# The residual of each FFN pair's first chunk turned by VectorE's 32x32 blocks and two transfers instead of by TensorE

## What is computed

```python
x = x + attn(layernorm(x) * ln_g + ln_b)     # q, k times a normalised sigmoid gate, relu()**2 + eps,
                                             # causal running sums k (x) v and k over the sequence
z = layernorm(x)                             # "z1" below; the part that the change is about
P = z @ U1                                   # 512 -> 128
H = gelu(P @ V1 + b1)                        # 128 -> 2048
x = x + (H @ U2) @ V2 + b2                   # 2048 -> 128 -> 512
```

## Time and profile before

| | us |
|---|---|
| median of 3 runs | 1702.19 (1701.56 to 1702.4) |
| the profiled execution | 1701.4 |
| its span, from the first to the last instruction | 1699.7 |
| PE busy | 1668.6 |
| DVE busy | 1437.1 |
| POOL busy | 880.5 |
| ACT busy | 629.6 |

### The profile page before, as it was taken

One profiled execution on the slowest core, in us unless ns is written; L12 is line 12 of the kernel. 1 busy time (PEld: TensorE's weight loads), 2 busy tenths in 40 slices (PEclk: granted clock), 3 DMA queues, 4 the chain that ended last, 5 costly groups with the idle time before them and its releaser, 6 DMA issues.

```text
span 1699.7 us, 39613 instructions
## 1 busy us (share of the span) xinstructions
PE 1668.6 (98%) x16221; PEld 1404.5 (83%) x16221; DVE 1437.1 (85%) x2223; ACT 629.6 (37%) x1178; POOL 880.5 (52%) x1026
## 2 busy tenths in 40 slices
PE   6899999999999999999999999999999999999997
PEld 4688888888888888888888888888888888888886
DVE  6888888888888888888888888888888888888885
ACT  4233334333433433433433333333333334334333
POOL 3355555555555555555555555555555555555540
PEclk9999999999999999999999999999999999999999
DMA  8323333333332233242243233333323333323310
GB/s 224 93 58 64 65 75 46 70 75 57 71 70 47 74 71 60 73 64 53 74 72 58 74 46 70 75 59 70 73 45 73 70 60 73 71 47 72 60 45 26
DMA packets 206324, 115.67 MB, mean 68 GB/s; under 512 B 151144, under 2 KB 161792, under 8 KB 206144
## 3 DMA queue, kind: packets, MB, share of 16 engines
q1 hardware_dynamic: 205280, 111.57, 31.6%
q10 hardware_dynamic: 864, 1.57, 0.4%
HBM read 79.38 MB, written 33.72 MB: 67 GB/s over the span
## 4 chain that ended last, share of the span: by engine, by line
PE 93%; DVE 3%; DMA 1%; issue 1%; SPq 1%; ACT 0%; POOL 0%; DVEq 0%; POOLq 0%
PE ps_a L849 11%; PE ps_a L850 10%; PE ps_a L851 10%; PE scores L849 8%; PE scores L851 8%; PE scores L850 8%; PE ps_h L849 4%; PE ps_h L850 4%; PE ps_h L851 4%; PE scores L980 4%; PE scores L1016 4%; PE ps_q L849 3%; PE ps_q L850 3%; PE ps_q L851 3%; PE scores L856 3%; PE scores L1010 2%
## 5 line engine op out<-in xcount | busy, mean ns | idle before, releaser
L447 POOL TENSOR_TENSOR h_lo<-h_full,h_hi 128x512 fp32r<-128x512 f32 x244 | 318.0, 1309 | 233.7 <-DVE h_hi L665 233.7
L849 PE MATMUL ps_a<-wx_hi,zt_hi 128*128 128x512 f32 x768 | 315.7, 411 | 6.6 <-DVE key_sums L787 4.2
L850 PE MATMUL ps_a<-wx_lo,zt_hi 128*128 128x512 f32 x768 | 305.1, 397 | 0.0
L851 PE MATMUL ps_a<-wx_hi,zt_lo 128*128 128x512 f32 x768 | 305.1, 397 | 0.0
L530 ACT ACTIVATE h_full<-ps_h,cols 128x256 f32<-128x256 f32 x512 | 204.0, 475 | 149.7 <-PE ps_h L851 149.6
L665 DVE CAST h_hi<-h_full 128x512 fp32r<-128x512 f32 x256 | 193.5, 766 | 22.9 <-ACT h_full L530 15.8
L849 PEld LDWEIGHTS ps_a<-wx_hi,zt_hi 128*128 128x128 f32 x768 | 145.3, 189 | 43.4 <-DVE zt_lo L620 7.4
L851 PEld LDWEIGHTS ps_a<-wx_hi,zt_lo 128*128 128x128 f32 x768 | 145.1, 189 | 35.6
L850 PEld LDWEIGHTS ps_a<-wx_lo,zt_hi 128*128 128x128 f32 x768 | 145.3, 189 | 28.7 <-issue 0.5
L541 ACT ACTIVATE query_t<-scores 128x512 f32<-128x512 f32 x64 | 38.3, 598 | 345.4 <-PE scores L856 345.4
L401 POOL TENSOR_TENSOR small<-moments,eps_col 128x1 f32<-128x1 f32 x64 | 12.2, 190 | 278.6 <-DVE moments L822 278.6
(11 more groups left out here) (156 smaller groups left out, 4133.2 us busy)
## 6 DMA issues: line engine op xcount, KB each, us to landing
xs<-L_attn_x SPq DMA_DIRECT2D x64, 256.0 KB, 4.1
key_blocks<-zs SPq DMA_DIRECT2D x64, 256.0 KB, 2.0
key_t<-key_blocks SPq DMA_DIRECT2D x256, 64.0 KB
out<-x1s SPq DMA_DIRECT2D x64, 256.0 KB, 2.1
xt<-x_turned SPq DMA_DIRECT2D x63, 256.0 KB, 4.2
key_sums<-carry_rows SPq DMA_DIRECT2D x60, 256.0 KB, 3.8
rows<-turned_rows SPq DMA_DIRECT2D x63, 64.0 KB, 4.5
x1s<-L_attn_W_gate SPq DMA_DIRECT2D x4, 256.0 KB, 4.1
```

The source lines that it names most:

```text
L447: E.tensor_tensor(h_lo[:, i % SLOTS, :], h_full[:, i % SLOTS, :], h_hi[:, i % SLOTS, :].bitcast(F32), ALU.subtract).then_inc(s["h_lo_ready ...
L849: E.matmul(ps, wh, mh, start=start and i == 0, stop=False)
L850: E.matmul(ps, wh, ml, start=False, stop=False)
L851: mm = E.matmul(ps, wl, mh, start=False, stop=stop and i == last)
```

## The change

In even steps, where d is the first chunk of a pair, TensorE no longer turns zs. VectorE turns zs by blocks of 32x32 into `queries`, which is free from the transposes of c until the query chain of n; SP stores that to a new buffer in memory (`res_dram`), waits, and gathers the blocks back into zs by four transfers of 128-byte pieces, so that the channels lie on the partitions. ScalarE makes x1t_hi from zs behind its gelus, and VectorE makes x1t_lo from zs behind the denominators and ahead of the first residual sum. New waits: VectorE's query chain waits for the store out of `queries`; SP waits for the block transposition and for its own store; ScalarE for the gathers. The key blocks go through `gate` instead of zs, and so the wait for their store moves from z1 (L830) to the denominators (L794). Odd steps keep the old way.

```diff
+    def pair(self, per=1):
+        return per * ((4 * self.p + self.off) // 2 + 1)
...
 # SP
             def step(p, b):
                 if isinstance(p, int) and 4 * p + b < 2:
                     load_tiles((range(FIRST + 6, FIRST + 9), range(FIRST + 9, len(tiles)))[b])
+                d = Chunk(p, b - 2)
+                if d.exists and d.half == 0:
+                    sp.wait_ge(s["res_ready"], d.pair())
+                    for j in range(HPG):
+                        wait(sp, res_in[j], d.pair(16) - 16)
+                    sp.dma_start(res_dram, queries[:, :]).then_inc(s["res_out"], 16)
+                    sp.wait_ge(s["res_out"], d.pair(16))
+                    for j in range(HPG):
+                        sp.dma_start(zs[j * HEAD:(j + 1) * HEAD, :].rearrange("d (f a t) -> d f a t", f=KT, t=HEAD),
+                                     res_dram.rearrange("(a d) (f j t) -> j d f a t", d=HEAD, f=KT, t=HEAD)[j])\
+                            .then_inc(res_in[j], 16)
...
-                    sp.dma_start(blocks_dram, zs[:, :]).then_inc(s["blocks_out"], 16)
+                    sp.dma_start(blocks_dram, gate[:, :]).then_inc(s["blocks_out"], 16)
 # ScalarE
-                if d.exists:
-                    act.wait_ge(s["tx_done"], d.done())
+                if d.exists and d.half:
+                    act.wait_ge(s["tx_done"], d.pair())
                     E.activation(x1t_hi[:, :, d.half * P:(d.half + 1) * P],
                                  ps_t[:, :].rearrange("p (k n) -> p k n", k=KT), ACT.Copy)\
                         .then_inc(s["x1t_hi_ready"], 1)
...
                     gelu(ffn, pairs[2])
                     gelu(ffn, pairs[3])
+                if d.exists and d.half == 0:
+                    for j in range(HPG):
+                        act.wait_ge(res_in[j], d.pair(16))
+                    E.activation(x1t_hi[:, :, 0:P], zs[:, :].rearrange("p (k n) -> p k n", k=KT), ACT.Copy)\
+                        .then_inc(s["x1t_hi_ready"], 1)
 # VectorE
+                def x1t_from_bank():
+                    if d.half:
+                        x1t_tail(ps_t)
+                def turn_residual():
+                    if d.exists and d.half == 0:
+                        dve.wait_ge(s["z1_ready"], d.done())
+                        if c.exists:
+                            dve.wait_ge(s["tq_done"], c.done())
+                        E.transpose(queries[:, :], zs[:, :]).then_inc(s["res_ready"], 1)
...
                         .then_inc(s["gate_evac"], 1)
+                    turn_residual()
...
                     squared_relu(n, s["key_done"], s["key_steps"], ps_b, KEY, keys[:, n.half, :],
-                                 x1t_tail)
+                                 x1t_from_bank)
...
+                    if d.exists and d.half == 0:
+                        dve.wait_ge(s["res_out"], d.pair(16))
                     squared_relu(n, s["query_done"], s["query_steps"], ps_a, QUERY, queries[:, :])
...
-                    if d.exists:
-                        dve.wait_ge(s["tx_done"], d.done())
-                    elif c.exists:
-                        dve.wait_ge(s["blocks_out"], c.done(16, 16))
-                    else:
-                        dve.wait_ge(s["tz_done"], 1)
-                    E.transpose(zs[:, :], keys[:, n.half, :]).then_inc(s["blocks_ready"], 1)
+                    E.transpose(gate[:, :], keys[:, n.half, :]).then_inc(s["blocks_ready"], 1)
...
                     dve.wait_ge(s["query_steps"], n.done(3, 3))
+                    dve.wait_ge(s["blocks_out"], n.done(16, 16))
                     E.scalar_tensor_tensor(out=gate[:, :], in0=queries[:, :], scalar=EPS, in1=key_sums[:, :],
...
+                if d.half == 0:
+                    x1t_tail(zs)
                 if c.exists:
                     dve.wait_ge(s["y_done"], c.done())
...
-                    if d.exists:
-                        dve.wait_ge(s["tx_done"], d.done())
+                    if d.exists and d.half:
+                        dve.wait_ge(s["tx_done"], d.pair())
...
-                    if n.exists:
-                        dve.wait_ge(s["blocks_out"], n.done(16, 16))
 # TensorE
-                if d.exists:
+                if d.exists and d.half:
                     pe.wait_ge(s["z1_ready"], d.done())
...
                     transpose4(zs, s["tx_done"])
...
-                    if d.exists:
+                    if d.exists and d.half:
                         pe.wait_ge(s["x1t_ready"], d.done())
```

More of the change, by code:

```diff
@@ L108, in block_kernel @@
 def block_kernel(nc, x, ln_g, ln_b, w_qkv, b_qkv, w_gate, b_gate, w_proj, b_proj,
-                 u1, v1, b1, u2, v2, b2, x_turned, out, carry_dram, rows_dram, blocks_dram):
+                 u1, v1, b1, u2, v2, b2, x_turned, out, carry_dram, rows_dram, blocks_dram, res_dram):
     ctx = ExitStack()
@@ L207, in block_kernel @@
             query_done query_steps value_done value_ready
-            sums_done den_steps blocks_ready blocks_out tq_done query_t_ready
+            sums_done den_steps blocks_ready blocks_out res_ready res_out tq_done query_t_ready
             scores_done probs_ready state_done state_ready ot_done ot_hi_ready ot_ready
@@ L215, in block_kernel @@
         xt_in = [sem(f"xt_in{i}") for i in range(4)]
+        res_in = [sem(f"res_in{j}") for j in range(HPG)]
         key_t_in = [sem(f"key_t_in{j}") for j in range(HPG)]
@@ L573, in step @@
                     gelu(ffn, pairs[3])
+                if d.exists and d.half == 0:
[3 more added lines that the diff above has]
+                        .then_inc(s["x1t_hi_ready"], 1)
+                if ffn.exists:
                     if b % 2 == 0:
@@ L677, in step, with x1t_tail @@
                 finishing = is_last(p)
-                def x1t_tail():
+                def x1t_tail(turned):
                     if d.exists:
@@ L682, in x1t_tail @@
                         part = slice(d.half * P, (d.half + 1) * P)
-                        E.tensor_tensor(x1t_lo[:, :, part], ps_t[:, :].rearrange("p (k n) -> p k n", k=KT),
+                        E.tensor_tensor(x1t_lo[:, :, part], turned[:, :].rearrange("p (k n) -> p k n", k=KT),
                                         x1t_hi[:, :, part].bitcast(F32), ALU.subtract).then_inc(s["x1t_ready"], 1)
+                def x1t_from_bank():
[7 more added lines that the diff above has]
+                        E.transpose(queries[:, :], zs[:, :]).then_inc(s["res_ready"], 1)
                 if n.exists:
@@ L704, in step @@
                     squared_relu(n, s["key_done"], s["key_steps"], ps_b, KEY, keys[:, n.half, :],
-                                 x1t_tail)
+                                 x1t_from_bank)
                 else:
-                    x1t_tail()
+                    turn_residual()
+                    x1t_from_bank()
                 if b % 2:
@@ L1070 @@
     blocks_dram = nc.dram_tensor("key_blocks", (P, DM), _mybir.dt.float32, kind="Internal").ap()
+    res_dram = nc.dram_tensor("residual_blocks", (P, DM), _mybir.dt.float32, kind="Internal").ap()
     rows_dram = nc.dram_tensor("turned_rows", (BATCHES, P), _mybir.dt.float32, kind="Internal").ap()
-    block_kernel(nc, *args, out, carry_dram, rows_dram, blocks_dram)
+    block_kernel(nc, *args, out, carry_dram, rows_dram, blocks_dram, res_dram)
     r = _run(nc, [arrays], core_ids=[0])
```

## The result

| | before | after |
|---|---|---|
| median us | 1701.93 | 1772.08 (4 runs, 1765.22 to 1777.74) |
| the profiled execution | 1701.4 | 1777.74 |
| its span | 1699.7 | 1776.0 |
| granted clock of TensorE, mean | 0.998 | 0.978 |

The ratio is 1.040, with a 95% interval of 1.038 to 1.042: 70 us slower, against a forecast of 4 us faster. The median before is that of the three runs on record ahead of the prediction and of one more.

What follows compares the result with a forecast made beforehand. TensorE, fed without a gap in the steady state, was taken as the bound: -14.0 for the transposes, +12.1 for the store's wait, -2.0 in the drain, -3.9 us in all, giving a median of 1698.3 us, range 1685 to 1711.

Steps and rivals of the forecast that it cites:

- The removed transposes: TensorE, first chunk of each pair: four transposes of zs and the refill go, 0.44 us a pair, 14.0 us in all.
- VectorE's transposition: VectorE turns zs into queries in 0.70 us, within 1.73 us of idling before ScalarE's sigmoid: costs nothing.
- the wait at the query chain: VectorE at L653 waits for the residual's store: about half a us in many even steps, 12.1 us given back.
- The drain: End of the kernel: no loads ahead, TensorE's wait for zs and the transposes go, 2.0 us won, 0 to 2.8.
- The gathers: Four transfers back into zs: 5.9 us, back by 796, wanted only after L794 at 802.35, so hidden.
- slower by VectorE's lateness: Rival: x1t_lo takes 1.28 instead of 0.69, 26.7 us given back, 28 of 30 steps stall, 1712.9 us; chance 0.20.
- The rival of the unhindered store: Rival: the residual's store is not held up by the loads, nothing is given back, 1686.2 us; chance 0.22.
- 19 times slower: Rival: gathers at 19 times a straight store, 38 us, delay x1t_lo and L815; about 2400 us; chance 0.01.
- The landing: The residual's store in the memory queue lands 5.0 us after xt's issue, bounds 4.8 and 5.14.
- the prediction's own rule: Even steps: L653 up to 0.19 us late costs nothing, each us beyond costs TensorE one; at 0.63 the gain is gone.
- its cases of 5.35 and 5.55: Values in us compared with the distance from xt's issue to L653: 5.35 gives back 21.3 us, 5.55 gives back 26.7.
- Nothing for the key blocks through gate: Key blocks' store out of gate, its wait moved to L794: hidden, no cost.

Runs made afterwards that it cites:

- the last run: Changed kernel with the residual's store issued ahead of loads xs and xt, and the first chunk's key blocks through zs again: 1690.96 us, ratio 0.9922.
- the two kernels that make it so: Changed kernel with the residual's store issued ahead of xs and xt (1692.6 us, 0.9941), or the residual turned into the masked scores' buffer (1694.17 us, 0.9956).
- the run without the collision: Changed kernel with GpSimd's key_lo, and the centring after it, started in even steps only after the query chain: 1709.12 us, ratio 1.0042.

## Why the prediction was wrong

**What held.** The removed transposes are worth 0.42 us a pair, taken at 0.44. VectorE's transposition is hidden (825.21, while it waits for the sigmoid). The store is held up by the loads, and the wait at the query chain is the largest new one of VectorE. The drain, taken at 2.0 us, gave 1.8 in the kernel after and 3.2 in the last run (from the last gate evacuation to the end 66.6 before, 64.8 and 63.4). The gathers stay hidden, each 2.6 us from issue to landing in the median. x1t_lo takes 0.68, taken at 0.69, so the rival "slower by VectorE's lateness" did not come about, though the direction did. The rival of the unhindered store gave 1686.2; the two kernels that make it so came to 0.9941 and 0.9956 of before, some 1692 to 1695, and without the loss at the start to 0.9922, 1688.9 of 1702.2. The prediction's "19 times slower" from the Trainium skill, VectorE: DVE Perf Modes, section "The three transpose paths", stands there under a condition that it left out, a large innermost stride at the destination. The gathers move pieces of 128 bytes that lie side by side at their destination, so nothing measured here tests it.

**A term that was short.** The landing was taken at 5.0 us after the issue of xt, with 5.14 as the upper bound. In the step shown VectorE goes on 5.50 after it (826.11 to 831.61), and the page's median has 4.8 after an issue that follows xt by 0.60. The bound came from one store in an odd step, issued 2.5 us behind xt, where this one follows it by 0.60. Put into the prediction's own rule, 0.45 more lies between its cases of 5.35 and 5.55, at about 23 us given back: -14 + 23 - 2 = +7 us, 1709. That is slower, and still inside the range.

**The step that failed** is the rule itself: "landing up to 0.19 after the old start of L653 costs nothing, each us beyond it costs TensorE one". It moves the query chain as a block of fixed length. It is not fixed: L656 and L660 are short only because they run before GpSimd's key_lo and centring, and they end as these begin. A chain that comes 1.1 us later lies beside both and takes 1.7 us more. Summed over 29 even steps (those with a load of xt, from the second on), the chain of the kernel after starts 21.2 us beyond the rule's limit, which is 6.11 after the gate evacuation (5.92 + 0.19); the masked scores start 57.0 us beyond theirs, 8.96 (8.77 + 0.19). In the run without the collision the same two sums are 18.0 and 17.2: there the chain passes its lateness on one for one, as the rule has it.

The time of that run, 1709.12 or +7 us, is also what the rule gives with the landing set right, but that is in part luck. Its profile is 11.6 us longer than that of before: 7.1 are lost by the fifth gate evacuation (121.30 against 114.21), where TensorE waits 6.0 us behind the key blocks' store, which the sum had at nothing; between there and the last gate evacuation it is 6.4 longer, where the rule gives -14 + 23 = 9; and 1.9 are won in the drain.

The remaining 63 us are what the rule left out: the longer chain, and the lower clock with the longer waits. These two can't be priced apart by that run: with the collision TensorE's wait fell from 52.3 to 12.7, and with the wait the mean clock rose to 0.994. What the clock costs by itself is only estimated, from the mean clock above: some 39 us less the 3 of before.

The prediction had the price in hand: it read 1.28 for L794 beside GpSimd. It asked this of the one instruction that it moved, x1t_lo, and not of those that its own new wait would push. GpSimd's timeline of the step, two rows, would have shown what they would lie beside. It had also cited the Trainium skill, SBUF — State Buffer, section "SBUF: two separate sides", by which a VectorE operation with two SBUF inputs and a GpSimd operation that reads SBUF shut each other out for a whole instruction. The trace agrees with that section: L679 and L683 go on as GpSimd's instruction ends and take 1.55 and 1.66, against means of 755 and 708 ns where the overlap is taken away.

**The clock** was not in the prediction at all. In the steady state before TensorE had no idle time, and the step of the earlier trace rows stood at 1.00, so no price could be read there. The trace of before does hold one sign, at its start: TensorE waits 4.24 us until 41.20, and the granted clock is 0.50 from 40.10 to 46.90.

**Nothing for the key blocks through gate** was wrong by the start: 2.5 us of TensorE in the first chunk, where the store stands behind the weights. In the profile of that part by itself the wait for the store comes once, and the steps behind the start last as long as before.

## What to carry over

When a wait pushes a chain of instructions, ask for each of them what it will lie beside at its new time, here on GpSimd: durations read at the old time hold only there. Put a transfer that somebody waits for ahead of those that nobody waits for, in the order of issue; here 2 us in the queue decided between 0.994 and 1.040. A slack of 0.2 us is no slack when what comes behind it grows with the lateness.

## What the runs showed of the hardware

- A VectorE instruction with two SBUF operands (128 x 512, 32 bits) that began beside a GpSimd instruction of the same size ended 0.55 us after it, twice in the step shown, and took 1.55 and 1.66 us instead of 0.75 and 0.70. The masked scores, with one operand in PSUM, took 2.25 beside both GpSimd instructions in the step of before (792.76 to 795.01), and 2.25 without them in the kernel after.
- In the kernel after, the granted clock fell to 0.50 around the end of 14 of 18 waits of TensorE of 1.77 to 2.65 us in mid-run, and with the masked scores made twice of 9 of 30 waits of 1.64 to 1.99. The mean clocks of 0.978 and 0.985 come to 39 and 27 us in the two kernels, estimates from above. Waits of 0.7 us on the mean in 30 steps left 0.996. Which waits are hit is open.
- A 256 KB store right behind two loads of that size lands 4.8 us after its issue in the median, ahead of them after 2.8, with one load ahead after 3.9.
